# Cross-attention with a gate: the low part of the transposed context by a negated ScalarE copy and an accumulating DMA

## The chip, the cores and the metric

The kernel runs on one core of one Trainium2 chip. The metric is the device time of one execution in microseconds. An engine works through its own list of instructions in order and waits on semaphores; TensorE multiplies matrices, VectorE (DVE), ScalarE (ACT) and GpSimd (POOL) work on rows, SP only issues DMAs. ACT and POOL can issue DMAs too.

## The reference

Float32 throughout. The bias b_gate and the weight norm_w are drawn values, not zeros and ones.

```python
# x: (8, 100, 1024), ctx: (8, 722, 512), W_mem: (1024, 512), W_gate: (1024, 2048)
memory_proj = einsum('bme,de->bmd', ctx, W_mem)
scores = einsum('bnd,bmd->bnm', x, memory_proj) / sqrt(1024)
attn = softmax(scores, axis=-1)
memory_context = einsum('bnm,bmd->bnd', attn, memory_proj)
gate_input = concatenate([x, memory_context], axis=-1)
gate = sigmoid(einsum('bnf,df->bnd', gate_input, W_gate) + b_gate)
fused = x + gate * memory_context
out = fused * rsqrt(mean(square(fused), axis=-1) + 1e-6) * norm_w
```

## The kernel before

**Split numbers.** Each float32 operand of a large matmul is held as two float32r tensors: `hi`, a ScalarE copy that rounds, and `lo`, the rest, which VectorE makes as original minus `hi` (the helper `minus`, L677 and L678, one line for all of them). A product is then three matmuls: hi hi, hi lo and lo hi. All operands stand transposed, with the dimension that is summed over on the partitions.

**Stages.** W_mem is moved to the side of x: first q = x W_mem, all 800 rows, so that the scores of batch b are q_b times the transposed context. Then eight attention steps, one per batch, each with a piece of other work for TensorE: one of the eight tiles of x W_gate (`gate_x`, recorded on L283). Then the projection of the attended context back by W_mem (`mc_block`), the gate's second half, and a normalisation at the end.

**A step on TensorE**, written out by hand (`step`, L336 to L388): wait for `ct_lo_done` 2b + 2 and for `qb_copied`; 24 matmuls of scores (L355) that read `ct_hi`, `ct_lo`; 4 of the 8 blocks of `gate_x`; six transposes of probabilities (L369); 3 blocks; 18 matmuls of probabilities with the untransposed context `cn_hi`, `cn_lo` (L379); 1 block; four transposes (L386). The first step cuts the blocks differently, 2, 3, 2 and 1, two of them ahead of its scores.

**A step on ScalarE** (L563 to L593), in order: exponential of the scores (L565), `w_hi` for the next gate tile (L489), the second part of `cn_hi` (L511, L512), `qb_hi` (L542), `pt_hi` of the transposed probabilities (L574, L576), then `split_ctxT(b + 1)`: after `scores_made` 2(b + 1) and, for each half s of two, after the load `ct_in[s]`, one copy of 128x1444 to `ct_hi` (L500). Then it waits for TensorE's `pc_made` and scales `pc` (L581), copies `q_hi` and the gate tile, and splits the first part of the next `cn`.

**A step on VectorE** (L747 to L774): the maxima of the scores, `qb_lo`, `w_lo`, `pt_lo`, the second part of `cn_lo`, then `split_ctxT(b + 1)`: two subtractions to `ct_lo`, then a copy of the gate tile, `q_lo`, and the first part of the next `cn_lo`.

**SP's queue** (`ahead`, L244 to L247) loads for the steps after: the weight tile that is two further (after `w_lo_done`), the two halves of the transposed context to `ct_stage` (L203, each after a count of `ct_lo_done`), and the untransposed one to `cn_stage` in three issues (L210, L214, L216, after `cn_lo_done`). `ct_stage`, `ct_hi` and `ct_lo` have one buffer each. POOL makes an identity at the start and, at the end, the roots `rms` (L912) and four diagonals (L917).

Of the kernel before, what the change touches and what calls it, by code (L numbers as in the profile page):

```python
# [1 line left out]

# [3 lines left out]
B, N, D = 8, 100, 1024  # L20
# [28 lines left out]
def build(nc, xT, ctxT, ctxN, w_mem, w_gate_x, w_mem_t, w_gate_mc, b_gate, norm_w, outT):  # L49
    F32, F32R = mybir.dt.float32, mybir.dt.float32r  # L50
    ALU, ACT, AX = mybir.AluOpType, mybir.ActivationFunctionType, mybir.AxisListType

    top = ExitStack()
    with top:  # L54
# [3 lines left out]
        def sem(name):  # L58
            return top.enter_context(nc.semaphore(name))
# [23 lines left out]
        with ExitStack() as attn:  # L83
            ct_stage = sb(attn, "ct_stage", [P, KC, M])
# [45 lines left out]
        w_hi_done, w_lo_done = sem("w_hi_done"), sem("w_lo_done")  # L130

        first_hi_done, first_lo_done = sem("first_hi_done"), sem("first_lo_done")
        ct_hi_done, ct_lo_done = sem("ct_hi_done"), sem("ct_lo_done")
        cn_hi_done, cn_lo_done = sem("cn_hi_done"), sem("cn_lo_done")
        q_hi_done, q_lo_done = sem("q_hi_done"), sem("q_lo_done")
        pt_hi_done, pt_lo_done = sem("pt_hi_done"), sem("pt_lo_done")
# [51 lines left out]
        @block.sync  # L188
        def _(sp):
            def load_x(k):  # L190
                sp.dma_start(acc[:, k, :], xT[k * P:(k + 1) * P, :]).then_inc(x_in[k], 16)

            def load_w(j, src, slot):

                if not isinstance(j, int) or j >= 2:
                    sp.wait_ge(w_lo_done, j - 1)
                sp.dma_start(w_stage[:, slot, :], src).then_inc(w_in[slot], 16)

            def load_ctxT(b, first=False):
                for s in range(2):  # L200
                    if not first:
                        sp.wait_ge(ct_lo_done, 2 * b - 1 + s)
                    sp.dma_start(ct_stage[:, 2 * s:2 * s + 2, :],  # L203
                                 ct_rows[bass.ds(b * C + s * 2 * P, 2 * P), :]
                                 .rearrange("(k p) m -> p k m", p=P)).then_inc(ct_in[s], 16)

            def load_ctx(b, first=False):
                if not first:
                    sp.wait_ge(cn_lo_done, 2 * b - 1)
                sp.dma_start(cn_stage[:, 0:3, :], cn_rows[bass.ds(b * M, 3 * P), :]  # L210
                             .rearrange("(t p) c -> p t c", p=P)).then_inc(cn_in[0], 16)
                if not first:
                    sp.wait_ge(cn_lo_done, 2 * b)
                sp.dma_start(cn_stage[:, 3:MT, :], cn_rows[bass.ds(b * M + 3 * P, (MT - 3) * P), :]  # L214
                             .rearrange("(t p) c -> p t c", p=P)).then_inc(cn_in[1], 16)
                sp.dma_start(cn_stage[0:ML, MT, :],  # L216
                             cn_rows[bass.ds(b * M + MT * P, ML), :]).then_inc(cn_in[1], 16)


            sp.dma_start(acc[:, 0, 0:H], xT[0:P, 0:H]).then_inc(x_first_in, 16)  # L220
            for i in range(2):
                cols = slice(i * C // 2, (i + 1) * C // 2)
                sp.dma_start(w_stage[:, 0, cols], w_mem[0][:, cols]).then_inc(w_first_in[i], 16)  # L223
            sp.dma_start(acc[:, 0, H:R], xT[0:P, H:R]).then_inc(x_in[0], 16)
            sp.dma_start(w_stage[:, 0, C:WB], w_mem[0][:, C:WB]).then_inc(w_in[0], 16)
            load_x(1)
            load_x(2)
            load_w(1, w_mem[1], 1)
            load_x(3)
            load_x(4)  # L230
            load_x(5)
            load_w(2, w_mem[2], 0)
            load_x(6)
            load_x(7)
            load_w(3, w_mem[3], 1)
            load_ctxT(0, first=True)
            load_ctx(0, first=True)
            sp.dma_start(bias_t[:, :], b_gate).then_inc(const_in, 16)
            sp.dma_start(norm_t[:, :], norm_w).then_inc(const_in, 16)
            load_w(J_GX, w_gate_x[0], 0)  # L240
            load_w(J_GX + 1, w_gate_x[1], 1)


            def ahead(b, slot):  # L244
                load_w(J_GX + 2 + b, wgx_rows[bass.ds((b + 2) * P, P), :], slot)
                load_ctxT(b + 1)
                load_ctx(b + 1)  # L247

            with sp.Fori(0, B // 2 - 1) as i:
                b = 2 * i  # L250
                ahead(b, 0)
                ahead(b + 1, 1)
            load_w(J_MC, w_mem_t[0], 0)
            load_ctxT(B - 1)
            load_ctx(B - 1)
            load_w(J_MC + 1, w_mem_t[1], 1)
            load_w(J_MC + 2, w_mem_t[2], 0)
            load_w(J_MC + 3, w_mem_t[3], 1)
            load_w(J_G2, w_gate_mc[0], 0)


            sp.wait_ge(mc_made, 1)
            sp.dma_start(x_again[:, :, :], xT.rearrange("(k p) r -> p k r", p=P)).then_inc(xa_in, 16)
            load_w(J_G2 + 1, w_gate_mc[1], 1)
            with sp.Fori(0, KD // 2 - 1) as i:
                for u in range(2):
                    load_w(J_G2 + 2 + 2 * i + u, wg2_rows[bass.ds((2 * i + u + 2) * P, P), :], u)
            with sp.Fori(0, KD // 2) as i:
                for u in range(2):
                    load_w(J_G2 + KD + 2 * i + u, wg2_rows[bass.ds((2 * i + u) * P, P), :], u)  # L270
            for args in SP_STORES:
                store(sp, *args)
            sp.wait_ge(stored, 16 * len(SP_STORES + ACT_STORES))
# [3 lines left out]
        def _(pe):  # L277
# [58 lines left out]
            def step(b, slot, cuts):  # L336
# [9 lines left out]
                    pe.wait_ge(w_lo_done, J_GX + 1 + b)  # L346
                    fill(0)

                pe.wait_ge(ct_lo_done, 2 * b + 2)
                pe.wait_ge(qb_copied, 2 * b + 2)  # L350
                for h in range(2):
                    at = h * (MH - 1)
# [129 lines left out]
        def _(act):  # L482
# [12 lines left out]
            def split_ctxT(b):  # L495
                if not isinstance(b, int) or b > 0:
                    act.wait_ge(scores_made, 2 * b)
                for s in range(2):
                    act.wait_ge(ct_in[s], 16 * b + 16)
                    nc.scalar.activation(ct_hi[:, 2 * s:2 * s + 2, :], ct_stage[:, 2 * s:2 * s + 2, :],  # L500
                                         ACT.Copy).then_inc(ct_hi_done, 1)

            def split_ctx(b, part):
                if part == 0:
# [171 lines left out]
        def _(dve):  # L676
            def minus(out, whole, hi):  # L677
                return nc.vector.tensor_tensor(out, whole, hi.bitcast(F32), ALU.subtract)  # L678
# [6 lines left out]
                dve.wait_ge(x_hi_done, k + 1)  # L685
                minus(act_lo[:, k, :], acc[:, k, :], act_hi[:, k, :]).then_inc(x_lo_done, 1)

            def split_ctxT(b):
                for s in range(2):
                    dve.wait_ge(ct_hi_done, 2 * b + s + 1)  # L690
                    minus(ct_lo[:, 2 * s:2 * s + 2, :], ct_stage[:, 2 * s:2 * s + 2, :],
                          ct_hi[:, 2 * s:2 * s + 2, :]).then_inc(ct_lo_done, 1)

            def split_ctx(b, part):
                dve.wait_ge(cn_hi_done, 2 * b + part + 1)
                if part == 0:
# [23 lines left out]
            split_x(6)  # L720
            split_x(7)
            split_w(3, 1)
            split_ctxT(0)
            split_ctx(0, 0)
            split_ctx(0, 1)
            split_w(J_GX, 0)
# [20 lines left out]
            def step(b, slot, more):  # L747
                for h in range(2):
                    dve.wait_ge(scores_made, 2 * b + h + 1)
                    nc.vector.reduce_max(top_score[:, h:h + 1], bank(h, MH + 1, N), AX.X).then_inc(top_found, 1)  # L750
                dve.wait_ge(top_found, 2 * b + 2)
                nc.vector.tensor_scalar(neg_top[:, :], top_score[:, 0:1], top_score[:, 1:2],  # L752
                                        -float(D) ** -0.5, ALU.max, ALU.mult).then_inc(neg_top_set, 1)
                if more:
                    copy_q(b + 1)
                split_w(J_GX + 1 + b, 1 - slot)
                dve.wait_ge(exp_done, b + 1)
                nc.vector.reciprocal(row_inv[:, :], row_sum[:, :]).then_inc(inv_set, 1)
                dve.wait_ge(pt_hi_done, b + 1)
                minus(pt_lo[:, 0:MT, :], bank(PTB, MT * N).rearrange("p (t n) -> p t n", n=N), pt_hi[:, 0:MT, :])  # L760
                minus(pt_lo[0:ML, MT, :], bank(PTB5, N, ML, KC * N), pt_hi[0:ML, MT, :]).then_inc(pt_lo_done, 1)
                if not isinstance(b, int) or b > 0:
                    split_ctx(b, 1)
                if more:
                    split_ctxT(b + 1)
                if more:
                    save_gate(b)
                dve.wait_ge(at_hi_done, b + 1)
                minus(q_lo[:, :, bass.ds(b * N, N)], bank(PTB5, KC * N).rearrange("p (c n) -> p c n", n=N),
                      q_hi[:, :, bass.ds(b * N, N)]).then_inc(at_lo_done, 1)  # L770
                if not more:
                    save_gate(b)
                if more:
                    split_ctx(b + 1, 0)  # L774
# [128 lines left out]
        def _(pool):  # L903
# [3 lines left out]
                                    base=0, pattern=[[-1, N]], channel_multiplier=1).then_inc(consts_set, 1)  # L907


            for g, (b0, n) in enumerate(GROUPS):  # L910
                pool.wait_ge(mean_copied, g + 1)
                nc.gpsimd.tensor_tensor(rms[:, b0:b0 + n], rms[:, b0:b0 + n], minus_half[:, 0:n],  # L912
# [35 lines left out]
```

## Time and profile before

| | us |
|---|---|
| median of 3 executions | 306.04 |
| lowest and highest | 305.05, 307.36 |
| span of the profiled execution, first to last instruction | 305.9 |
| TensorE busy in it | 293.2 |
| VectorE busy | 183.1 |
| ScalarE busy | 157.4 |
| mean granted clock of TensorE, share of full speed | 0.982 |

The profile gives the span of its execution and no other time of it; the median stands 0.14 us beside it. Matmuls overlap in the pipeline, so the busy time of TensorE says that it is seldom idle, not that it is at its peak. Spans of one instruction are in ns, starts and stretches in us from the start of the span.

### The profile page before, as it was taken

To read this page: it belongs to the slowest core of one execution; us is meant where nothing else is said; L and a number is where in the kernel's file an instruction comes from. 1 tells how busy PE (TensorE), PEld (TensorE's weight loads), DVE (VectorE), ACT (ScalarE), POOL (GpSimd) and SP (SyncE) were. 2 spreads that over 40 slices of the span, in tenths; PEclk is the share of its full clock that TensorE was granted. 3 is DMA by queue.
4 is the path that set the end of the run, shared out by engine and by line. 5 is a ranking of instruction groups with operands and counts; after the bars stand their busy time and mean duration, and the time that the engine had idled before them with its cause. 6 is when DMAs were issued, how large, how long until landed. Compare 5 with 4: busy or idle time off the path is not lost.

```text
span 305.9 us, 4511 instructions
## 1 busy us (share of the span) xinstructions
PE 293.2 (96%) x1658; PEld 281.0 (92%) x1658; DVE 183.1 (60%) x267; ACT 157.4 (51%) x225; POOL 7.9 (3%) x13
## 2 busy tenths in 40 slices
PE   8899999999999999999999999999999999799961
PEld 8899999898989989898998989999999999799961
DVE  3657564557585656758565525334367776748895
ACT  4547345564563936356393506543545566336640
POOL 0000000000000000000000000000000000700010
PEclk9999999999999999999999999999999999979995
DMA  6996291644928386472834011192143334305118
GB/s 204 406 394 221 88 354 47 229 112 121 292 94 291 119 242 213 142 263 97 289 119 159 20 50 69 58 411 98 69 140 137 92 116 137 113 31 181 60 54 268
DMA packets 21198, 50.47 MB, mean 165 GB/s; under 512 B 1712, under 2 KB 5296, under 8 KB 21184
## 3 DMA queue, kind: packets, MB, share of 16 engines
q1 hardware_dynamic: 20096, 49.46, 46.9%
q10 hardware_dynamic: 1088, 0.82, 0.8%
q8 instruction: 9, 0.15, 0.2%
q14 instruction: 5, 0.04, 0.0%
HBM read 47.00 MB, written 3.28 MB: 164 GB/s over the span
## 4 chain that ended last, share of the span: by engine, by line
PE 91%; POOL 2%; DMA 2%; DVE 1%; issue 1%; SPq 1%; ACT 0%; POOLq 0%; DVEq 0%
PE ps L283 67%; PE ps L379 11%; PE ps L355 11%; DMA acc<-xT 2%; PE ps L369 1%; POOL rms_diag L917 1%; POOL rms L912 1%; PE ps L386 1%; PE ps L456 1%; DVE acc L853 1%; DVE act_lo L678 0%; ACT act_hi L493 0%; SPq L223 0%; POOLq L54 0%; PE ps L447 0%
## 5 line engine op out<-in xcount | busy, mean ns | idle before, releaser
L283 PE MATMUL ps<-act_hi,w_hi 128*128 128x400 f32 (+1 forms) x328 | 99.0, 345 | 1.2 <-DVE act_lo L678 1.2
L283 PE MATMUL ps<-act_lo,w_hi 128*128 128x400 f32 (+1 forms) x328 | 98.1, 342 | 0.0
L283 PE MATMUL ps<-act_hi,w_lo 128*128 128x400 f32 (+1 forms) x328 | 98.0, 342 | 0.0
L283 PEld LDWEIGHTS ps<-act_hi,w_hi 128*128 128x128 f32 x328 | 60.9, 190 | 2.7 <-issue 1.5
L283 PEld LDWEIGHTS ps<-act_lo,w_hi 128*128 128x128 f32 x328 | 61.6, 190 | 0.0
L283 PEld LDWEIGHTS ps<-act_hi,w_lo 128*128 128x128 f32 x328 | 61.5, 189 | 0.0
L678 DVE TENSOR_TENSOR w_lo<-w_stage,w_hi 128x1024 fp32r<-128x1024 f32 (+2 forms) x34 | 39.5, 1160 | 26.2 <-ACT w_hi L489 25.5
L489 ACT ACTIVATE w_hi<-w_stage 128x1024 fp32r<-128x1024 f32 x31 | 32.8, 1058 | 37.0 <-PE ps L283 36.6
L678 DVE TENSOR_TENSOR cn_lo<-cn_stage,cn_hi 128x1536 fp32r<-128x1536 f32 (+2 forms) x24 | 28.5, 1217 | 5.2 <-ACT cn_hi L508 5.2
L678 DVE TENSOR_TENSOR ct_lo<-ct_stage,ct_hi 128x1444 fp32r<-128x1444 f32 x16 | 25.8, 1654 | 0.5 <-ACT ct_hi L500 0.5
L581 ACT ACTIVATE pc<-ps,row_inv 100x512 f32<-100x512 f32 x8 | 5.5, 687 | 34.0 <-PE ps L379 34.0
L500 ACT ACTIVATE ct_hi<-ct_stage 128x1444 fp32r<-128x1444 f32 x16 | 21.7, 1410 | 0.0
L355 PE MATMUL ps<-ct_hi,qb_hi 128*100 128x362 f32 x64 | 21.3, 333 | 0.0
L355 PE MATMUL ps<-ct_hi,qb_lo 128*100 128x362 f32 x64 | 21.0, 328 | 0.0
L355 PE MATMUL ps<-ct_lo,qb_hi 128*100 128x362 f32 x64 | 21.0, 328 | 0.0
L565 ACT ACTIVATE probs<-ps,neg_top 100x722 f32<-100x722 f32 x8 | 6.9, 866 | 27.2 <-DVE neg_top L752 27.2
L678 DVE TENSOR_TENSOR act_lo<-mc,act_hi x8 | 7.9, 992 | 20.8 <-ACT mc L614 20.8
L379 PE MATMUL ps<-cn_lo,pt_hi 128*100 128x512 f32 (+1 forms) x48 | 18.9, 394 | 0.0
L379 PE MATMUL ps<-cn_hi,pt_hi 128*100 128x512 f32 (+1 forms) x48 | 18.8, 392 | 0.0
L379 PE MATMUL ps<-cn_hi,pt_lo 128*100 128x512 f32 (+1 forms) x48 | 18.8, 392 | 0.0
L823 DVE TENSOR_TENSOR gate<-ps,acc 128x400 f32<-128x400 f32 (+1 forms) x17 | 9.3, 549 | 14.0 <-PE ps L283 13.9
L283 PE MATMUL ps<-q_hi,w_hi 128*128 128x400 f32 x64 | 17.5, 344 | 0.0
(71 smaller groups left out, 351.6 us busy)
## 6 DMA issues: line engine op xcount, KB each, us to landing
ct_stage<-ctxT SPq DMA_DIRECT2D x16, 722.0 KB, 9.5
w_stage<-w_gate_mc SPq DMA_DIRECT2D x16, 512.0 KB, 3.5
cn_stage<-ctxN SPq DMA_DIRECT2D x8, 768.0 KB, 5.8
cn_stage<-ctxN SPq DMA_DIRECT2D x8, 512.0 KB
w_stage<-w_gate_x SPq DMA_DIRECT2D x8, 512.0 KB, 8.3
x_again<-xT SPq DMA_DIRECT2D x1, 3200.0 KB, 12.3
acc<-xT SPq DMA_DIRECT2D x7, 400.0 KB, 7.8
w_stage<-w_mem_t SPq DMA_DIRECT2D x4, 512.0 KB, 5.6
```

Of the source, the lines that this page charges most:

```text
L283: done = nc.tensor.matmul(o, wgt, stream[h][part], start=first and wgt is wh and part == 0, stop=last and wgt is wl)
L355: done = nc.tensor.matmul(bank(h, MH + 1, N), lhs[:, k, :], rhs[:, k, at:at + MH + 1], start=k == 0 and part == 0, stop=k == KC - 1 and pa ...
L369: done = nc.tensor.transpose(o, probs[:, t * P:t * P + rows], ident[:, :])
L379: done = nc.tensor.matmul(bank(PCB, C, N), lhs[0:rows, t, :], rhs[0:rows, t, :], start=t == 0 and part == 0, stop=t == MT and part == 2)
L386: done = nc.tensor.transpose(bank(PTB5, N, P, c * N), pc[:, c * P:(c + 1) * P], ident[:, :])
L456: done = nc.tensor.matmul(bank(RIB[g], N, P, i * N), ones[:, :], rms_diag[:, b0 + i, :], start=True, stop=True)
L489: nc.scalar.activation(w_hi[slot][:, :], w_stage[:, slot, :], ACT.Copy).then_inc(w_hi_done, 1)
L500: nc.scalar.activation(ct_hi[:, 2 * s:2 * s + 2, :], ct_stage[:, 2 * s:2 * s + 2, :], ACT.Copy).then_inc(ct_hi_done, 1)
L565: nc.scalar.activation(probs[:, :].rearrange("p (h m) -> p h m", h=2), scores, ACT.Exp, bias=neg_top[:, :], scale=float(D) ** -0.5, accum_ ...
L581: nc.scalar.activation(pc[:, :], bank(PCB, C, N), ACT.Copy, scale=row_inv[:, :]).then_inc(pc_scaled, 1)
L678: return nc.vector.tensor_tensor(out, whole, hi.bitcast(F32), ALU.subtract)
L823: nc.vector.tensor_tensor(g, bank(G2B + slot, part.stop - part.start, P, part.start), rows, ALU.add).then_inc(gate_summed, 1)
```

## The change

ScalarE writes each half of the transposed context twice: rounded to `ct_hi`, and negated and rounded to `ct_lo`. A DMA of POOL's queue then adds `ct_stage` onto `ct_lo`, in SBUF, so that `ct_lo` becomes the original minus its rounded value. VectorE's two subtractions per batch are gone. TensorE's scores wait for both DMAs of their batch, and SP's loads of `ct_stage` wait for the DMA of their half. POOL's sixteen DMAs, each behind its wait, stand before its work at the end.

```diff
-        ct_hi_done, ct_lo_done = sem("ct_hi_done"), sem("ct_lo_done")
+        ct_neg_done, ct_lo_in = sem("ct_neg_done"), [sem(f"ct_lo_in{s}") for s in range(2)]
...
             def load_ctxT(b, first=False):
                 for s in range(2):
                     if not first:
-                        sp.wait_ge(ct_lo_done, 2 * b - 1 + s)
+                        sp.wait_ge(ct_lo_in[s], 16 * b)
...
-                pe.wait_ge(ct_lo_done, 2 * b + 2)
+                for s in range(2):
+                    pe.wait_ge(ct_lo_in[s], 16 * b + 16)
                 pe.wait_ge(qb_copied, 2 * b + 2)
...
                 for s in range(2):
                     act.wait_ge(ct_in[s], 16 * b + 16)
-                    nc.scalar.activation(ct_hi[:, 2 * s:2 * s + 2, :], ct_stage[:, 2 * s:2 * s + 2, :],
-                                         ACT.Copy).then_inc(ct_hi_done, 1)
+                    half = slice(2 * s, 2 * s + 2)
+                    nc.scalar.activation(ct_hi[:, half, :], ct_stage[:, half, :], ACT.Copy).then_inc(ct_neg_done, 1)
+                    nc.scalar.activation(ct_lo[:, half, :], ct_stage[:, half, :], ACT.Copy,
+                                         scale=-1.0).then_inc(ct_neg_done, 1)
...
-            def split_ctxT(b):
-                for s in range(2):
-                    dve.wait_ge(ct_hi_done, 2 * b + s + 1)
-                    minus(ct_lo[:, 2 * s:2 * s + 2, :], ct_stage[:, 2 * s:2 * s + 2, :],
-                          ct_hi[:, 2 * s:2 * s + 2, :]).then_inc(ct_lo_done, 1)
-
...
-            split_ctxT(0)
...
-                if more:
-                    split_ctxT(b + 1)
...
+            for b in range(B):
+                for s in range(2):
+                    half = slice(2 * s, 2 * s + 2)
+                    pool.wait_ge(ct_neg_done, 4 * b + 2 * s + 2)
+                    pool.dma_start(ct_lo[:, half, :], ct_stage[:, half, :],
+                                   accum_op=ALU.add).then_inc(ct_lo_in[s], 16)
```

## Rows read from the trace of the kernel before

**Rows 1.** The page: span, then busy us (share of the span) and instructions.

```profile
span 305.9 us, 4511 instructions
...
PE 293.2 (96%) x1658; PEld 281.0 (92%) x1658; DVE 183.1 (60%) x267; ACT 157.4 (51%) x225; POOL 7.9 (3%) x13
```

**Rows 2.** The page: the chain that ended last, share of the span by engine.

```profile
PE 91%; POOL 2%; DMA 2%; DVE 1%; issue 1%; SPq 1%; ACT 0%; POOLq 0%; DVEq 0%
```

**Rows 3.** The chain in order of time: start us, us, what; L355 opens a step.

```profile
43.49 3.96 PE ps L355 x24
...
59.04 3.98 PE ps L355 x24
...
130.17 3.98 PE ps L355 x24
...
147.91 4.12 PE ps L355 x24
...
165.78 3.98 PE ps L355 x24
```

**Rows 4.** Timeline of ACT in one step: start us, us, what [idle before <-releaser].

```profile
139.82 2.71 ACT L500 ACTIVATE ct_hi<-ct_stage 128x1444 fp32r<-128x1444 f32 x2
146.51 0.69 ACT L581 ACTIVATE pc<-ps,row_inv 100x512 f32<-100x512 f32 x1 [3.97 <-PE ps L379]
```

**Rows 5.** Timelines of DVE and SP in the same step.

```profile
142.46 3.22 DVE L678 TENSOR_TENSOR ct_lo<-ct_stage,ct_hi 128x1444 fp32r<-128x1444 f32 x2
...
134.53 0.37 SPq L210 DMA_DIRECT2D cn_stage<-ctxN  x1
142.71 0.37 SPq L214 DMA_DIRECT2D cn_stage<-ctxN  x1
...
143.76 0.35 SPq L197 DMA_DIRECT2D w_stage<-w_mem_t  x1
```

**Rows 6.** The page: groups of instructions, xcount | busy us, mean ns | idle before.

```profile
L678 DVE TENSOR_TENSOR ct_lo<-ct_stage,ct_hi 128x1444 fp32r<-128x1444 f32 x16 | 25.8, 1654 | 0.5 <-ACT ct_hi L500 0.5
L500 ACT ACTIVATE ct_hi<-ct_stage 128x1444 fp32r<-128x1444 f32 x16 | 21.7, 1410 | 0.0
```

**Rows 7.** Windows: stretch, length, busy PE, PEld, DVE, ACT, POOL; clock, DMA share, GB/s.

```profile
130.17:147.91 17.74, 17.74 (x102) 16.34 (x101) 11.31 (x16) 9.97 (x14) 0.00 (x0) 1.00 0.58 190
...
144.00:146.00 2.00, 2.00 (x10) 1.46 (x9) 1.68 (x2) 0.00 (x0) 0.00 (x0) 1.00 0.70 229
...
148.00:150.00 2.00, 2.00 (x13) 1.99 (x13) 0.87 (x2) 1.96 (x3) 0.00 (x0) 1.00 1.04 325
```

**Rows 8.** Timeline of ACT in the prologue and in the first step.

```profile
24.94 2.71 ACT L500 ACTIVATE ct_hi<-ct_stage 128x1444 fp32r<-128x1444 f32 x2
...
37.51 2.15 ACT L552 ACTIVATE q_hi<-ps 128x400 fp32r<-128x400 f32 x4 [3.78 <-PE ps L283]
...
51.89 2.71 ACT L500 ACTIVATE ct_hi<-ct_stage 128x1444 fp32r<-128x1444 f32 x2
57.64 0.69 ACT L581 ACTIVATE pc<-ps,row_inv 100x512 f32<-100x512 f32 x1 [3.04 <-PE ps L379]
```

**Rows 9.** The tile `ct_stage`: time from issue to landing of its loads.

```profile
DMA to landing us min/median/max: 4.1/9.5/10.3
```

**Rows 10.** DMA issues: KB each, median us to landing.

```profile
cn_stage<-ctxN SPq DMA_DIRECT2D x8, 512.0 KB
...
cn_stage<-ctxN SPq DMA_DIRECT2D x8, 164.0 KB
outT<-acc SPq DMA_DIRECT2D x4, 200.0 KB, 2.3
```

**Rows 11.** Windows at the end of the kernel.

```profile
295.00:298.00 3.00, 0.96 (x8) 0.87 (x8) 2.62 (x9) 1.49 (x4) 0.85 (x1) 1.00 0.36 136
...
300.00:302.00 2.00, 0.80 (x4) 0.55 (x3) 1.59 (x5) 0.00 (x0) 0.00 (x0) 0.50 0.93 300
```

**Rows 12.** Timeline of POOL: its first work after the prologue.

```profile
260.41 2.41 POOL L912 TENSOR_TENSOR rms<-rms,minus_half 100x4 f32<-100x4 f32 x1 [258.98 <-DVE rms L839]
```

## The prediction

> **What bounds the kernel now.** I read the busy times of the page first: TensorE is busy 293.2 of 305.9 us, VectorE 183.1, ScalarE 157.4 [rows 1]. The chain that ended last agrees: 91% of it is TensorE, VectorE holds 1% [rows 2]. So 26 us less on VectorE is worth nothing by itself; what counts is whether TensorE ever waits for `ct_lo`. Next comes the chain in order of time. The eight attention steps begin their scores (L355) at 43.49, 59.04, 76.78, ... 165.78, the last six gaps between starts sum to 106.74 us, 17.79 each [rows 3], and between two starts TensorE has no hole, 17.74 us busy in 17.74 [rows 7]. Call the start of a step's scores T. Then I read, for the step with T = 130.17, what the other engines do relative to T, since the scores of the next batch (T + 17.74) now wait for two DMA landings instead of for VectorE.
>
> Before the change the wait is slack: ScalarE writes both halves of `ct_hi` from 139.82, which is T + 9.65, in 2.71 us [rows 4], VectorE's two subtractions run 142.46 to 145.68, and the scores start at 147.91: 2.23 us to spare [rows 5].
>
> **What is removed.** Sixteen subtractions of 1654 ns, 25.8 us of VectorE [rows 6]. In a step nothing of VectorE ends a wait of TensorE, its part of the chain is the epilogue's, so the gain is 0. The cover is TensorE itself, against whose full step VectorE has 11.31 us [rows 7].
>
> **What ScalarE gets.** Sixteen more copies of the shape of `ct_hi`, 1410 ns each [rows 6]: 22.6 us. Four in a row instead of two: starts are 2.71 - 1.41 = 1.30 apart, so 3 x 1.30 + 1.41 = 5.31 us, ending at T + 14.96. ScalarE then sat idle 3.97 us until TensorE had made `pc`, in the first step 3.04 [rows 4, 8]; the extra 2.60 fits in both. In the prologue the two copies start at 24.94; the first work that the scores need after them, `q_hi`, found ScalarE idle for 3.78 us [rows 8]. Cost 0. Without that cover it would be 2.60 us a step, 18.
>
> **What the DMA path costs.** The second accumulating DMA can be issued only at T + 14.96 (the first at T + 9.65 + 2.71 = T + 12.36). If A is the time from then to its landing, the next scores start at T + 14.96 + A, and TensorE's order is fixed, so nothing of its other work can fill the hole. For the six steps with a gap known: 6 x (14.96 + A) - 106.74 = 6A - 16.98. For the second step of all: ScalarE starts at 51.89 [rows 8], is through at 57.20, against a start of scores at 59.04: A - 1.84. Together the seven waits come to **7A - 18.8 us**, nothing if A is under 2.7. The first batch is free: its copies end at 24.94 + 5.31 = 30.25 and its scores start at 43.49.
>
> The trace has no accumulating DMA and none of POOL's queue. Bounds for A from the nearest rows: the load of the same tensor, of the same 722 KB, takes 4.1 us at the least, 9.5 median, 10.3 at the most from issue to landing [rows 9]; stores of 200 KB take 2.3 us [rows 10], a quarter of the bytes, so no row speaks for 2.7 us at 722 KB. Which end? The DMA engines are not empty at that moment. SP issues 512 and 164 KB of `cn_stage` one behind the other from 142.71, and a weight, again 512 KB, at 143.76, T + 12.5 to T + 13.6 [rows 5, 10], and the engines go from a busy share of 0.70 to 1.04 at 325 GB/s [rows 7]. None of these issues moves, as VectorE's `cn_lo` that releases them keeps its place. So both accumulations fall into the one busy stretch. At copy cost, 1188 KB of loads and 1444 KB of accumulation are 2.70 MB; at 325 GB/s that is 8.3 us from T + 12.5, so T + 20.8: A = 5.8, the least a shared queue gives. The load of the next `ct_stage` half, freed when the first accumulation lands, comes in beside the second one and takes half of the rate. I therefore take the contended row, A = 9.5: 7 x 9.5 - 18.8 = 47.7 us, and 305.9 + 47.7 = 353.6.
>
> **The clock.** A hole of 9.5 - 2.8 = 6.7 us per step is new. At the end of this trace TensorE is busy 0.96 of 3 us, and then its granted clock falls to 0.50 of full speed, the 1.2 GHz level [rows 11]; in the steps it is 1.00 [rows 7]. After each hole the scores, 3.98 us [rows 3], may run at that level. Bounds: 0 and 3.98 us a step. I take 1.0, a quarter of the doubling, because the row shows that a fall comes only some microseconds into low activity and nothing shows how fast it comes back: 7 us. **Sum 353.6 + 7 = 360.6; I say 360.** Span and median agree within 0.14 us (305.9 and 306.04), so no correction is due.
>
> **The buffers.** `ct_stage` is free not at T + 15.5 but when the accumulations land, about T' - 3 and T' (T' is the next T). Queued behind these two waits on SP are only `cn_stage`'s loads. `cn_stage`'s first was issued at 134.53, T + 4.36, waiting for VectorE [rows 5], so it isn't moved. The late `ct_stage` halves land at worst 10.3 us after T', and ScalarE wants the first at T' + 9.65 and the second at T' + 12.3 with a first half issued earlier. Just in time: 0. Behind the sixteen waits on POOL stands only the `rms` work of the end, first needed at 260.41 [rows 12], 76 us after the last step: 0.
>
> **A rule against the change.** The rows bound A by copies only. In the Trainium skill, Collectives: The Full Stack, section "The bandwidth ceiling: the fold count and why AG ≠ RS ≠ AR", says that an adding transfer reads two sources for each write and so reached half of the rate of a plain one. No run here shows it yet. By the contended copy row the sum is 360.6; by the rule it is the 385 to 392 of the second rival, which is worked out there from rows.
>
> **Rivals.**
> - *Hidden after all (not slower).* One mechanism: SBUF to SBUF, without HBM, the accumulation lands within 2.7 us of its issue. Then TensorE never waits: 305.9 us. It decides at A = 2.7 (3.1 for 1%). Against it: 2.3 us for 200 KB, and the busy DMA engines.
> - *Double traffic.* Each accumulated byte moves twice over the engines: 1188 + 2 x 1444 = 4076 KB, 4.17 MB, at 325 GB/s 12.8 us, landing at T + 25.3 at the least; with half a rate lost to the reload of `ct_stage` for some 4 us, T + 28. A = 13: 7 x 13 - 18.8 = 72, plus 7 to 14 for the clock: 385 to 392.
> - *Light traffic.* the engines turn from SP's queue to POOL's often enough that the accumulation, with longer rows (5776 bytes against the 2048 of `cn_stage`), is served mostly ahead of the loads; A is 4.1 to 6: 9.9 to 23 us, 316 to 329. For it: the 4.1 us row.
> - *A ring.* Accumulation is slow enough, A over 16, that the loads freed by it come late for ScalarE as well; each step then costs load plus copies plus accumulation, over 10.3 + 5.3 + 16 = 32 us: 7 x (32 - 17.8) = 99, above 400.
>
> **How the numbers follow.** Forecast (A of 7 to 11 and some clock loss, 336 to 378): 0.42. Double traffic: 0.27. Light traffic: 0.20. Ring: 0.07. Hidden: 0.04. The likeliest gives 360. The range is 325 to 400: outside remain hidden (0.04), the lighter third of light traffic (0.07), and the ring with the far end of double traffic (0.09). Changes of less than 1%, 3 us, can't be told from none by a measurement of this kernel. Slower by over 1% holds in all cases but hidden: 0.95; within 1%: 0.04; faster by over 1%: 0.01, since no case gives TensorE less work.
>
> **What the profile after would show.** If I am right: TensorE idle before L355 in seven steps, released by the DMA `ct_lo<-ct_stage`, 6 to 8 us each, and accumulations that land 7 to 11 us after their issue; TensorE's busy time about the same, or higher where the granted clock dips after the holes; VectorE down by 26 us, ScalarE up by 22.6, its idle time before L581 shorter by 2.6 a step; DMA issues of POOL x16. The sum is wrong if those DMAs land in under 6 or over 11 us. The clock term is wrong if the clock stays 1.00, or if it costs over 2 us a step. If ScalarE waits for `ctxT`, the ring is true, and my "just in time" was not.

## The result and the profile after

The changed kernel takes 387.65 us (median of 4, 386.51 to 388.38) against 306.51 of the kernel before (median of 4): a ratio of 1.264, 95% interval 1.260 to 1.269. The prediction was 360 us, with 325 to 400 as its range. The direction, the place and the form of the cost were right; the time is that of the rival called double traffic (385 to 392), though not by that rival's terms, as the part behind the experiments says.

The page of the changed kernel, busy times and the chain that ended last, against [rows 1, 2]:

```profile
span 384.7 us, 4537 instructions
...
PE 307.8 (80%) x1658; PEld 293.2 (76%) x1658; DVE 159.2 (41%) x251; ACT 178.5 (46%) x241; POOL 21.9 (6%) x29
...
PE 62%; DMA 21%; ACT 10%; issue 4%; POOL 2%; DVE 1%; POOLq 0%; DVEq 0%; ACTq 0%
```

VectorE has lost 24 us of work and ScalarE gained 21; TensorE gained 15 us of busy time for the same 1658 matmuls, which is the slower clock. A fifth of the chain is now DMA. The list of waits (engine, line, whom it waited for: us in total, times, longest us) names the hole:

```profile
PEld ps L342 <- issue: 66.7, 7, 10.5
PE ps L342 <- DMA ct_lo<-ct_stage: 59.2, 6, 10.4
...
PE ps L342 <- issue: 6.1, 1, 6.1
```

Seven holes ahead of the scores (L342 here, L355 before), 59.2 + 6.1 = 65.3 us. The 6.1, for which this view names nobody, are the second step's: its second DMA, issued at 56.3, landed 7.6 us later, 0.1 us ahead of the scores. The chain in order of time, one step of it, against [rows 3, 4]:

```profile
94.54 5.51 PE ps L342 x24
100.05 4.35 PE ps L269 x24
104.40 0.53 PE ps L356 x6
...
105.43 0.24 ACT pt_hi L565
105.67 1.30 ACT ct_hi L488
106.98 1.29 ACT ct_lo L489
108.27 1.30 ACT ct_hi L488
109.58 1.31 ACT ct_lo L489
110.89 0.28 issue
111.17 12.20 DMA ct_lo<-ct_stage
123.37 0.23 issue
123.60 6.27 PE ps L342 x24
...
244.81 5.48 PE ps L342 x24
```

The step takes 29.06 us where it took 17.79. The four ScalarE copies come in a row as costed, 5.3 us with the last one's full length; then POOL picks up the signal (0.28), the DMA lands after 12.20, and TensorE starts 0.23 later. The windows of the same hole in the step before (columns as in [rows 7]) show full DMA engines and a clock that falls while TensorE is idle:

```profile
86.00:88.00 2.00, 0.00 (x0) 0.00 (x0) 1.21 (x2) 1.05 (x1) 0.00 (x0) 0.80 0.99 300
88.00:90.00 2.00, 0.00 (x0) 0.00 (x0) 0.84 (x1) 0.00 (x0) 0.00 (x0) 0.50 0.99 209
...
94.50:96.00 1.50, 1.46 (x5) 1.40 (x6) 0.00 (x0) 0.00 (x0) 0.00 (x0) 0.50 0.35 96
96.00:98.00 2.00, 2.00 (x10) 1.91 (x9) 0.00 (x0) 0.00 (x0) 0.00 (x0) 0.64 0.94 358
98.00:100.00 2.00, 2.00 (x14) 1.99 (x13) 0.53 (x1) 0.00 (x0) 0.00 (x0) 1.00 1.00 364
```

So the scores start at 1.2 GHz, 5 matmuls in 1.5 us, and come back to 2.4 GHz only after some 3 us. The DMA queues (packets, MB, share of 16 engines' span) and issues (KB, median us to landing):

```profile
q1 hardware_dynamic: 20096, 49.46, 38.0%
q0 software_dynamic: 2304, 11.83, 15.5%
...
ct_lo<-ct_stage POOLq DMA_DIRECT2D x16, 722.0 KB, 10.5
```

What SP issues around the same hole (timeline of SP: start us, us, what) shows, beside the second part of `cn_stage` and the weight, one neighbour more, which the prediction foresaw and didn't price in its sum:

```profile
108.46 0.37 SPq L200 DMA_DIRECT2D cn_stage<-ctxN  x1
109.02 0.27 SPq L202 DMA_DIRECT2D cn_stage<-ctxN  x1
109.56 0.35 SPq L183 DMA_DIRECT2D w_stage<-w_gate_x  x1
119.12 4.79 SPq L189 DMA_DIRECT2D ct_stage<-ctxT  x2
```

The first accumulation of the batch lands just ahead of 119.12 and so releases the load of the first half of the next `ct_stage`, 722 KB, 4.25 us before the second accumulation lands at 123.37.

A share times the span is engine time. For the loads it is 0.380 x 384.7 / 49.46 = 2.96 us per MB, for the accumulations 0.155 x 384.7 / 11.83 = 5.04 us per MB, 1.70 times as much.

### The profile page after: what moved, and what is told of

It is laid out like the page before. It is cut to its first block, busy times and chain, and to the rows that moved or that the text cites. A ratio compares the mean times of both kernels' runs of the same rounds, so it can differ in the third digit from the quotient of the medians.

```text
span 384.7 us, 4537 instructions
## 1 busy us (share of the span) xinstructions
PE 307.8 (80%) x1658; PEld 293.2 (76%) x1658; DVE 159.2 (41%) x251; ACT 178.5 (46%) x241; POOL 21.9 (6%) x29
## 3 DMA queue, kind: packets, MB, share of 16 engines
q1 hardware_dynamic: 20096, 49.46, 38.0%
q0 software_dynamic: 2304, 11.83, 15.5%
## 4 chain that ended last, share of the span: by engine, by line
PE 62%; DMA 21%; ACT 10%; issue 4%; POOL 2%; DVE 1%; POOLq 0%; DVEq 0%; ACTq 0%
PE ps L269 45%; DMA ct_lo<-ct_stage 21%; PE ps L342 13%; ACT ct_lo L489 4%; ACT ct_hi L488 4%; PE ps L366 1%; PE ps L283 1%; PE ps L356 1%; POOL rms L900 1%; POOL rms_diag L905 1%; PE ps L443 1%; DVE acc L833 1%; ACT pt_hi L565 0%; DVE w_lo L667 0%; ACT w_hi L476 0%
## 5 line engine op out<-in xcount | busy, mean ns | idle before, releaser
L342 PE MATMUL ps<-ct_hi,qb_hi 128*100 128x362 f32 x64 | 28.3, 443 | 65.4 <-DMA ct_lo<-ct_stage 59.2
L342 PEld LDWEIGHTS ps<-ct_hi,qb_hi 128*100 128x100 f32 x64 | 15.2, 237 | 67.3 <-issue 66.7
L732 DVE TENSOR_REDUCE top_score<-ps 100x1 f32<-100x362 f32 x16 | 8.6, 534 | 81.6 <-PE ps L342 81.6
L667 DVE TENSOR_TENSOR cn_lo<-cn_stage,cn_hi 128x1536 fp32r<-128x1536 f32 (+2 forms) x24 | 28.5, 1217 | 10.5 <-ACT cn_hi L497 10.5
L342 PE MATMUL ps<-ct_lo,qb_hi 128*100 128x362 f32 x64 | 27.4, 428 | 0.0
L342 PE MATMUL ps<-ct_hi,qb_lo 128*100 128x362 f32 x64 | 26.9, 420 | 0.0
L894 POOL DMA_DIRECT2D ct_lo<-ct_stage x16 | 14.0, 873 | 217.8 <-ACT ct_lo L489 217.8
L489 ACT ACTIVATE ct_lo<-ct_stage 128x1444 fp32r<-128x1444 f32 x16 | 22.5, 1404 | 0.0
L726 DVE COPY acc<-ps 128x400 f32<-128x400 f32 (+1 forms) x8 | 4.6, 573 | 37.6 <-PE ps L269 37.6
L366 PE MATMUL ps<-cn_hi,pt_hi 128*100 128x512 f32 (+1 forms) x48 | 18.8, 392 | 0.0
L366 PE MATMUL ps<-cn_hi,pt_lo 128*100 128x512 f32 (+1 forms) x48 | 18.8, 392 | 0.0
## 6 DMA issues: line engine op xcount, KB each, us to landing
ct_lo<-ct_stage POOLq DMA_DIRECT2D x16, 722.0 KB, 10.5
```

The source lines that it names most:

```text
L342: done = nc.tensor.matmul(bank(h, MH + 1, N), lhs[:, k, :], rhs[:, k, at:at + MH + 1], start=k == 0 and part == 0, stop=k == KC - 1 and pa ...
L366: done = nc.tensor.matmul(bank(PCB, C, N), lhs[0:rows, t, :], rhs[0:rows, t, :], start=t == 0 and part == 0, stop=t == MT and part == 2)
L489: nc.scalar.activation(ct_lo[:, half, :], ct_stage[:, half, :], ACT.Copy, scale=-1.0).then_inc(ct_neg_done, 1)
L726: nc.vector.tensor_copy(acc[:, bass.ds(b, 1), H:R].rearrange("p k r -> p (k r)"), bank(GXB + 1, H)).then_inc(gx_saved, 1)
L894: pool.dma_start(ct_lo[:, half, :], ct_stage[:, half, :], accum_op=ALU.add).then_inc(ct_lo_in[s], 16)
```

## The experiments

The theory after the result: TensorE's time grows by seven holes, each set by the landing of the last accumulating DMA, plus the slow clock behind it; the landing is long because an adding DMA costs more engine time per byte than a copy and shares the engines with the loads of `cn_stage` and of the weight (SP's load of the next `ct_stage` half, seen above, was not singled out). Rivals: ScalarE's 22 us; a cost of POOL's queue or of the type conversion; a clock loss that only hides behind the next landing; a fixed latency that no neighbour changes. Ratios are to the kernel before in the same job, with 95% intervals.

**1. ScalarE's part alone.** Negated copies stay, VectorE subtracts again over `ct_lo`, POOL issues nothing.

```diff
+            def split_ctxT(b):      # VectorE
+                for s in range(2):
+                    dve.wait_ge(ct_neg_done, 4 * b + 2 * s + 2)
+                    minus(ct_lo[:, 2 * s:2 * s + 2, :], ct_stage[:, 2 * s:2 * s + 2, :],
+                          ct_hi[:, 2 * s:2 * s + 2, :]).then_inc(ct_lo_done, 1)
```

> The ScalarE part alone: the sixteen negated copies stay, VectorE subtracts again over them, no DMA of POOL. Theory (the extra 22.5 us of ScalarE are hidden; all of the loss is the DMA wait and the clock after it): within 1% of before, 305 to 309 us, since VectorE's second subtraction now ends near T + 16.7, 1 us before the scores. Rival (ScalarE's 2.6 us a step are paid): 315 to 325 us.

Measured 307.26 us, ratio 1.002 (0.999 to 1.005). ScalarE's extra work is hidden, as the prediction had it at 0. The run takes nothing off VectorE, so it doesn't test that part.

**2. A plain copy in place of the adding one.** This kernel leaves the addition out, and its output differs for that.

```diff
-                    pool.dma_start(ct_lo[:, half, :], ct_stage[:, half, :],
-                                   accum_op=ALU.add).then_inc(ct_lo_in[s], 16)
+                    pool.dma_start(ct_lo[:, half, :], ct_stage[:, half, :]).then_inc(ct_lo_in[s], 16)
```

> The changed kernel with the sixteen DMAs as plain copies of the same bytes in the same queue, so that ct_lo holds the context itself and the low part is left out of the computation. Theory (an adding DMA moves each byte more than once): the second landing of a step falls from 12.2 us to 8 to 9, the DMA engines' time in that queue from 59 us to 30 to 40, and the kernel takes 355 to 368 us. Rival (it is the queue, POOL's descriptors or the loads beside it, and the adding is free): landing 11.5 to 12.5 us, time 383 to 389 us.

Measured 359.23 us, ratio 1.173 (1.167 to 1.178). Queues, and two landings in the chain, of this kernel:

```profile
q1 hardware_dynamic: 20096, 49.46, 41.0%
q0 software_dynamic: 2304, 11.83, 9.8%
...
101.12 8.83 DMA ct_lo<-ct_stage
...
154.44 9.07 DMA ct_lo<-ct_stage
```

The same 2304 packets and 11.83 MB take 0.098 x 357.4 = 35.0 us of the engines where adding took 59.6: 2.96 us per MB, exactly the loads' price. The second landing in steps three to eight falls from about 12.2 us to between 8.1 and 9.1. The adding costs 28 us of the 81, its part in the clock included; the other 53 are there with a copy. The shortest landing is 3.4 us for the copy and 5.5 for the addition.

**3. The type conversion.** The DMA sees `ct_lo` as float32.

```diff
-                    pool.dma_start(ct_lo[:, half, :], ct_stage[:, half, :],
+                    pool.dma_start(ct_lo[:, half, :].bitcast(F32), ct_stage[:, half, :],
                                    accum_op=ALU.add).then_inc(ct_lo_in[s], 16)
```

> The changed kernel with ct_lo seen as float32 by the DMA, so that source and destination have one type. Theory (two reads per write): no change, 385 to 390 us. Rival (the type conversion between float32 and float32r is what costs): landing falls to 8 or 9 us, 355 to 368 us.

Measured 388.65 us (386.74 and 390.55), ratio 1.269 (1.260 to 1.278): no change. The conversion costs nothing that shows.

**4. TensorE kept busy in the hole**, in steps two to eight.

```diff
+                if not isinstance(b, int) or b > 0:
+                    for _ in range(160):
+                        nc.tensor.matmul(bank(7, P), idle_work[:, :], idle_work[:, :], start=True, stop=True)
```

> The changed kernel with 160 small bfloat16 matmuls of zeros in the hole ahead of the wait for the DMAs in steps two to eight, about 9 us of TensorE's time that was idle. Theory (the clock is a cost of its own, the scores take 44.4 us in seven steps where 27.9 were needed): the granted clock stays near 1.00 in the steps, the scores take 4.0 us each, and the time falls by 12 to 16.5 us to 371 to 376 us. Rival (the loss is hidden behind the next DMA wait, since the transfers set the pace by themselves): 384 to 389 us.

Measured 376.40 us (375.36 and 377.43), ratio 1.229 (1.222 to 1.236), 11.3 us less than the changed kernel and just above the theory's 371 to 376. The chain of this kernel shows the same landing and shorter scores:

```profile
68.67 4.01 PE ps L345 x24
...
111.58 12.07 DMA ct_lo<-ct_stage
123.88 4.22 PE ps L345 x24
```

The mean granted clock rose from 0.888 to 0.985, and the scores of steps two to seven went from 38.9 to 25.1 us together: 13.8 us. The missing 2.5 us are in the second step, whose hole was only 6.1 us: filled with about 9 us of matmuls, its scores began 24.48 us after the first step's, against 21.71, though their DMA had landed over 2.5 us before. So the clock is a term of its own, 16.5 us over all seven steps by the chain (44.4 us of scores less seven times 3.98), of which 11.3 were won back in the time.

**5. The neighbours moved away.** The second part of `cn_stage` and the weight are issued after both landings. So is the first half of the next `ct_stage` (`load_ctxT`), which stands behind the same wait now; what was expected doesn't name it.

```diff
             def ahead(b, slot, w=None):
+                for s in range(2):
+                    sp.wait_ge(ct_lo_in[s], 16 * b + 16)
...
+                    load_ctx_rest(b)         # cn_stage, 512 and 164 KB
                 load_ctxT(b + 1)
+                load_w(J_GX + 2 + b, ..., slot)
```

> The changed kernel with SP's other loads moved: the second part of cn_stage and the weight tile are issued after both accumulations of the batch have landed, instead of just as they start. Theory (half of the landing time is sharing the DMA engines with these 1188 KB): the second landing falls from 12.2 to 7 to 8 us, the holes to about 5 us, and the time to 350 to 362 us. Rival (the two accumulations alone fill the engines, or the loads are now late for ScalarE): 375 us or more, in the second case with ScalarE waiting for cn_stage or ct_stage.

Measured 352.24 us, ratio 1.152 (1.147 to 1.157). The second landing is 6.64 to 6.66 us in all of steps three to eight, a little below the 7 to 8 that were expected:

```profile
105.82 6.64 DMA ct_lo<-ct_stage
```

The order of SP's issues alone was worth 35 us. For the `ct_stage` half only the second step says something, since no `cn_stage` and no weight is in flight there: its second landing is 7.6 us in the changed kernel and in runs 3 and 4, 6.6 in this run and in run 11, which both hold the half back. But run 12 holds it back too and has 7.6 there, so a share of about 1 us is likely and not shown.

**6. One accumulating DMA per batch.** The first half by DMA, the second by VectorE.

```diff
+                pool.wait_ge(ct_neg_done, b + 1)
+                pool.dma_start(ct_lo[:, 0:2, :], ct_stage[:, 0:2, :], accum_op=ALU.add).then_inc(ct_lo_in, 16)
...
+                minus(ct_lo[:, 2:4, :], ct_stage[:, 2:4, :], ct_hi[:, 2:4, :]).then_inc(ct_lo_done, 1)
```

> Only the first half of the transposed context by the negated copy and the accumulating DMA, the second by VectorE's subtraction. The last DMA is issued at T + 12.4 instead of T + 15, and there is one in place of two. Theory (landing time follows the bytes ahead and beside): landing 8 to 9.5 us, so a hole of 2.6 to 4 us in each of seven steps and some clock loss: 325 to 345 us. Rival (a fixed 10 us or more per accumulating DMA): a hole of over 5 us, above 350 us.

Measured 354.97 us, ratio 1.161 (1.156 to 1.166). A miss: half of the accumulated bytes were gone and the landing was still 10.4 us, not 8 to 9.5. The rival's numbers held here, yet its reason, a fixed 10 us, falls with the next run.

**7. One DMA and no neighbours.** Runs 5 and 6 together.

> Both: one accumulating DMA per batch, and no other load beside it. Theory: it lands 5.5 us after its issue, at T + 17.9 against a start of scores at T + 17.75, so the holes are 0 to 0.5 us and the clock stays: 305 to 312 us. Rival (an accumulating DMA can't land in 5.5 us in a step, or its waits cost by themselves): holes of 1.5 us and more, 317 us or more.

Measured 318.90 us, ratio 1.043 (1.039 to 1.048): a miss of the theory, within the rival's 317 and more, and with its holes of about 1.5 us. But the rival's first reason falls, since the landing is 5.4 us as the theory said:

```profile
ct_lo<-ct_stage POOLq DMA_DIRECT2D x8, 722.0 KB, 5.4
...
ACT cn_hi L506 <- DMA cn_stage<-ctxN: 9.8, 6, 2.4
```

What the expectation left out is the second line, from the waits: `cn_stage`, issued late, reaches ScalarE late, 9.8 us over six steps, and `ct_hi` stands behind it in ScalarE's list. 12.36 + 0.28 + 5.45 + 0.23 and a wait of 1.6 are 19.9 us for a step; from the second step on the starts of the scores lie 19.4 to 20.5 apart.

**8. Which neighbour.** As run 6, the weight tile alone moved.

```diff
             def ahead(b, slot, w=None):
-                load_w(J_GX + 2 + b, ..., slot)
                 load_ctxT(b + 1)
+                load_w(J_GX + 2 + b, ..., slot)
```

> The kernel with one accumulating DMA per batch, and of its two neighbours only the weight tile of 512 KB is moved behind the landing; the 676 KB of cn_stage are still issued 0.1 us after the DMA. Landing was 10.4 us with both neighbours and 5.4 us with neither. Theory (the delay follows the bytes of the neighbours, 5.0 us for 1188 KB): 5.4 + 5.0 x 676 / 1188 = 8.2 us, the holes 2.2 us shorter than with both, the time 330 to 340 us. Rival (it is the transfer issued first, cn_stage, that holds the engines, and the weight adds nothing): landing 10 us or more, 350 us or more.

Measured 353.81 us, ratio 1.157 (1.147 to 1.166), landing 10.5 us: the theory of bytes fails and the rival's numbers hold. The windows of this kernel say why; DMA share is the last but one number, and the DMA that was issued at 97.00 landed at 107.50:

```profile
100.00:102.00 2.00, 2.00 (x14) 1.79 (x12) 0.00 (x0) 0.69 (x1) 0.00 (x0) 1.00 1.03 220
...
103.50:104.00 0.50, 0.00 (x0) 0.00 (x0) 0.49 (x1) 0.50 (x1) 0.00 (x0) 1.00 0.10 20
104.00:104.50 0.50, 0.00 (x0) 0.00 (x0) 0.00 (x0) 0.50 (x1) 0.00 (x0) 1.00 0.14 31
104.50:105.50 1.00, 0.00 (x0) 0.00 (x0) 0.83 (x1) 0.13 (x1) 0.00 (x0) 1.00 0.14 31
...
106.50:107.50 1.00, 0.00 (x0) 0.00 (x0) 0.00 (x0) 0.00 (x0) 0.00 (x0) 0.50 0.13 40
```

From 103.5 on the share is 0.10 to 0.14, two engines of sixteen, for 4 us. TensorE's scores wait all that time. The only transfer of an odd shape is the last part of `cn_stage`, 82 rows, 164 KB. In the Trainium skill, DMA: Bandwidth & Descriptors, section "Why a DMA increments its semaphore by 16 and not by 1", a transfer uses the largest number of engines up to 16 that divides its row count, which for 82 is 2; the trace's 0.13 agrees.

**9. The 82 rows moved, the weight in place.**

```diff
+                if b > 0:
+                    sp.wait_ge(ct_lo_in, 16 * b + 16)
+                    load_ctx_tail(b)     # 82 rows, 164 KB
                 load_ctxT(b + 1)
```

> One accumulating DMA per batch; of its three neighbours only the 164 KB load of the last 82 rows of cn_stage is moved behind the landing. In the kernels with one accumulating DMA the DMA engines' busy share fell to 0.10 to 0.14, two of sixteen, for the last 1.5 to 4 us before the landing. Theory (the 82 rows sit on two engines, and the accumulation's share on these two comes out last): landing falls from 10.4 to 7 to 8.2 us, although only 164 of 1188 KB are gone, and the time from 355 to 328 to 342 us. Rival (bytes in all count): landing 9.7 us, 348 us or more.

Measured 341.53 us, ratio 1.115 (1.108 to 1.123), 13.4 us less than run 6 for 164 KB, just within the theory's range of times and clear of the rival's 348; the landing, 9.5 us in the median, is not within the theory's 7 to 8.2 and is near the rival's 9.7. In the last step the weight stands behind the moved load as well, and the DMA lands in 6.95 us there.

**10. The 82 rows and the weight moved.**

> The same with the weight tile moved too, so that 512 KB of cn_stage alone stay beside the DMA. Moving the weight while the 82 rows stayed gained nothing. Theory (with the two slow engines out of the way the bytes of the weight count): landing 6 to 6.8 us, holes of about 1.5 us, 315 to 326 us. Rival (the engines of the 82 rows aren't the cause): landing 9 us or more, 345 us or more.

Measured 325.81 us, ratio 1.064 (1.054 to 1.074), just within the theory's range; landing 7.3 us, half a microsecond above the theory's.

Runs 6 to 10 together, landing of the one DMA by what is issued beside it. The lines of runs 6, 9 and 10:

```profile
ct_lo<-ct_stage POOLq DMA_DIRECT2D x8, 722.0 KB, 10.4
...
ct_lo<-ct_stage POOLq DMA_DIRECT2D x8, 722.0 KB, 9.5
...
ct_lo<-ct_stage POOLq DMA_DIRECT2D x8, 722.0 KB, 7.3
```

| beside it | landing, us | time, us |
|---|---|---|
| nothing (7) | 5.4 | 318.9 |
| 512 KB of `cn_stage` (10) | 7.3 | 325.8 |
| 512 KB and the weight (9) | 9.5 | 341.5 |
| 512 KB and the 82 rows (8) | 10.5 | 353.8 |
| all three (6) | 10.4 | 355.0 |

Each evenly spread 512 KB adds 1.9 to 2.2 us; with the 82 rows the landing is 10.4 to 10.5 with the weight or without. This reads as two ends, the full engines' and that of the two slow ones, of which the later counts, so that taking one away shows little while the other is there. A run with the 82 rows alone beside the DMA is missing. The time of run 7 also holds ScalarE's wait for the moved `cn_stage`; in runs 9 and 10 ScalarE has no such wait.

**11. The changed kernel with the 82 rows moved**, both halves by DMA.

> The changed kernel itself, both halves by accumulating DMAs, with only the 164 KB load moved behind the landings. Theory: the second landing falls from 12.2 to 9 to 10.5 us, since the two accumulations and two loads of 512 KB still fill all engines for some 10 us, and the time from 388 to 366 to 378 us. Rival (with two accumulations all sixteen engines are full to the end and the two slow ones don't matter): 383 to 389 us.

Measured 369.61 us, ratio 1.207 (1.200 to 1.214), 18 us less than the changed kernel and within the theory's range. The second landing is 10.2 to 10.6 us in steps three to seven and 7.9 in the last; one of the five:

```profile
107.83 10.54 DMA ct_lo<-ct_stage
```

Not all of the 18 us is the 82 rows': their load waits for both landings, so the `ct_stage` half behind it in SP's list is held back as well, and in the last step the weight too. That the landing stays above 10 us without the 82 rows fits two accumulations that keep all engines full. Run 9 is the cleaner figure for the 82 rows, 13.4 us with one accumulation, the last step's weight included.

**12. Neighbours moved and TensorE kept busy.** Run 5 with 80 small matmuls in each hole.

> Loads moved behind the landings, and 80 small matmuls of zeros in each hole, about 4.5 us. The scores of steps two to eight took 41.6 us there where 27.9 were needed. Theory (landing time and clock are two separate terms that add): the second landing stays at 6.7 us, the scores go back to 4.0 to 4.2 us, and the time falls from 352 us to 338 to 342 us. Rival (one hides behind the other): 348 us or more.

Measured 350.04 us (348.82 and 351.27), ratio 1.144 (1.132 to 1.157), only 2 us less, so the rival was right on the time. Landings of the second DMA are 6.65 us in five steps of seven and 7.55 and 8.40 in the others, and a matmul of the scores that reads `ct_lo` went from 408 to 337 ns in the mean. The chain and the waits of this kernel show where the gain went:

```profile
161.85 7.97 DMA cn_stage<-ctxN
...
ACT cn_hi L508 <- DMA cn_stage<-ctxN: 8.7, 6, 2.4
```

With the scores faster, ScalarE comes to the deferred load before it has landed, 8.7 us over six steps against 1.0 in run 5, and the two longer landings cost 2.7 us. The filler didn't outlast the first hole here: TensorE then idled for 1.6 us more. So in the order of run 5 the clock loss mostly hid behind that load; why two landings came out longer stays open.

No kernel of these beats the one before: TensorE had no hole in its steps [rows 7], so nothing taken off VectorE there can pay.

## Why the prediction was right in direction and short in size

By its own signs of being wrong, a landing over 11 us and a clock cost over 2 us a step, two of its terms failed while its mechanism held.

- **VectorE's 25.8 us worth nothing; ScalarE's 22.6 us free.** ScalarE's part is right by run 1. No run takes the subtractions off by themselves; VectorE's part rests on [rows 7], where TensorE never waits in a step. POOL's waits ahead of `rms`: free too, as from the start of the eighth scores to the end both kernels take the same, 139.9 us now and 140.1 before.
- **The sum 7A - 18.8.** Right. With the measured second landings, 7.6 in the first of the seven steps and 12.20, 12.20, 12.24, 12.76, 12.04 and 12.24 after it, it gives 81.3 - 18.8 = 62.5 us. Two hand-overs that it left out, 0.28 to POOL and 0.23 to TensorE, are 3.6 us over seven steps. With 16.5 of clock that is 82.6; the span grew by 78.8. Of the difference, 1.2 us is that the first scores began earlier in this execution, at 42.32 instead of 43.49; the rest is not accounted for.
- **A = 9.5. This term was mis-sized:** 11.6 in the mean, 14.8 us in the sum. The contended row was that of a copy, and a copy it predicts well: run 2 has 8.1 to 9.1. What it can't hold is the engine time of adding, 1.70 times a copy's.
- **The double traffic rival** hit the time by luck in part: it had A = 13 and a factor of 2, both too high (11.6 and 1.70), and left out the hand-overs; its 7 to 14 us for the clock were too low. The rule of the Trainium skill that the prediction set against its row (Collectives: The Full Stack, section "The bandwidth ceiling: the fold count and why AG ≠ RS ≠ AR"), two reads per write and half of the rate, is borne out in direction, with 1.70 where it has 2.
- **"Both accumulations fall into the one busy stretch."** Right, and worth 35 us by run 5, the `ct_stage` half included, which the prediction saw coming beside the second one. But the share was priced as if all sixteen engines did every transfer. With the 164 KB of 82 rows beside it the DMA came out last on two of them: 13.4 us by run 9, at most 18 by run 11.
- **The clock at 1.0 us a step. Mis-sized:** 2.4 us, 16.5 in all, inside the bounds of 0 and 3.98. The quarter rested on nothing but that a fall takes time; the holes were longer than 6.7 us, 9.3 in the mean, and the scores after them run slow for some 3 us.
- **`ct_stage` just in time for ScalarE.** Right: in the changed kernel ScalarE has no wait for it, and the ring did not form.
- **Light traffic and hidden.** Both fall. Light traffic's A of 4.1 to 6 is met only by an accumulation with no neighbour, 5.4 us, and that is still twice the 2.7 at which the wait would vanish; one DMA with no neighbour still cost 4% (run 7).

## What to carry to other kernels

Before work is handed to a DMA, write down the time from its latest possible issue to the first reader: here 2.7 us against 5.4 for the transfer alone and 12.2 with its neighbours, and no saving on an engine that has slack could pay for that. Price an adding DMA by more than the row of a copy, and count everything that another queue issues at the same moment, since it shares the engines. Look for a neighbour whose row count divides badly: it occupies few engines for long (here two of sixteen), and a transfer that is spread over all of them waits for those few. And before an experiment moves one load, list what stands behind it in the same queue: that moves too.

## What the runs showed of the hardware that was not expected

- Adding in a DMA, SBUF to SBUF, 722 KB: 5.04 us of all engines per MB against 2.96 for the copy; landing 5.4 against 3.4 us at the least; POOL's issue 0.86 against 0.53 us (changed kernel and run 2).
- The conversion to float32r added nothing measurable to it (388.65 and 387.65 us).
- With a load of 82 rows, 164 KB, in flight, two of sixteen engines stayed busy (share 0.10 to 0.14) up to 4 us after the others had finished (run 8), and the landing of another queue's DMA went from 7.3 (run 10) to 10.5 us.
- In the changed kernel, after holes of 6 to 10 us the 24 matmuls of the scores took 5.5 to 6.95 us where 3.98 were needed.
